# A gated cross-attention layer with a routed FFN: the end of the kernel joined into its last batch

## What is computed

```python
x = x + tanh(g_xattn) * attention(layernorm(x), ctx, ctx, mask, Wq, ..., Wo, bo)
def ffn(x):                              # x is layernorm(x) of the line above
    indices = argmax(softmax(x @ Wr + br))
    out = 0
    for i in range(8):
        xi = x * (indices == i)
        out += relu(xi @ W1[i] + b1[i]) @ W2[i] + b2[i]
    return out
x = x + tanh(g_ffn) * ffn(layernorm(x))
```

## Time and profile before

| what | value |
|---|---|
| time, three executions | 391.19, 392.97, 394.4 us (median 392.97) |
| the profiled execution: time | 391.81 us |
| its span, first to last instruction | 390.0 us |
| PE busy | 358.8 us (92% of the span) |
| DVE, ACT, POOL busy | 277.4, 247.4, 193.7 us |
| granted TensorE clock, mean over the span | 0.973 of full speed |

### The profile page before, as it was taken

One profiled execution on the slowest core, in us unless ns is written; L12 is line 12 of the kernel. 1 busy time (PEld: TensorE's weight loads), 2 busy tenths in 40 slices (PEclk: granted clock), 3 DMA queues, 4 the chain that ended last, 5 costly groups with the idle time before them and its releaser, 6 DMA issues.

```text
span 390.0 us, 11299 instructions
## 1 busy us (share of the span) xinstructions
PE 358.8 (92%) x2829; PEld 289.4 (74%) x2829; DVE 277.4 (71%) x1300; ACT 247.4 (63%) x908; POOL 193.7 (50%) x373
## 2 busy tenths in 40 slices
PE   3969998999999999999999999999999978759991
PEld 2847777677877787787778778877877757659991
DVE  3289993988598959868895989598856654645661
ACT  1767874687586758766875886677745424536670
POOL 7047363456537634673564566446643522253553
PEclk9999999999999999999999999999999975989997
DMA  7898201001100200030003002000000037333320
GB/s 211 200 366 209 87 26 60 3 2 53 61 0 0 84 27 0 0 111 0 0 2 109 0 0 90 34 0 0 0 27 3 3 114 239 115 97 90 90 60 12
DMA packets 20552, 25.21 MB, mean 65 GB/s; under 512 B 3545, under 2 KB 16677, under 8 KB 20528
## 3 DMA queue, kind: packets, MB, share of 16 engines
q1 hardware_dynamic: 18544, 19.40, 16.8%
q0 software_dynamic: 1984, 5.53, 3.9%
HBM read 18.48 MB, written 6.90 MB: 65 GB/s over the span
## 4 chain that ended last, share of the span: by engine, by line
PE 82%; DVE 4%; issue 3%; DMA 3%; ACT 3%; another core or an unknown queue 1%; DVEq 1%; SPq 1%; POOL 1%; ACTq 0%; POOLq 0%
PE ps_kv L1158 16%; PE ps_o L1158 14%; PE ps_s L1158 13%; PE ps_t L1231 12%; PE ps_w L1158 9%; PE ps_q L1158 8%; PE ps_t L1158 7%; DVE masked L752 1%; ACT prob L557 1%; DMA sorted_rows<-rows,slot_i 1%; DMA bias_rows<-in_L_ffn_b 1%; PE ps_s L1436 1%; ACT hidden L656 1%; PE ps_w L1263 1%
## 5 line engine op out<-in xcount | busy, mean ns | idle before, releaser
L422 POOL TENSOR_SCALAR prob<-prob,row_inv 128x128 f32<-128x128 f32 (+1 forms) x256 | 104.7, 428 | 138.9 <-DVE row_inv L765 138.9
L557 ACT ACTIVATE prob<-masked,neg_max 128x128 f32<-128x128 f32 (+1 forms) x256 | 113.4, 444 | 68.0 <-DVE neg_max L752 68.0
L752 DVE CUSTOM_DVE_ANT_0 masked<-ps_s,mask_now 128x128 f32<-128x128 f32 (+1 forms) x256 | 78.9, 353 | 23.8 <-PE ps_s L1158 19.7
L771 DVE COPY prob_T<-ps_t 128x384 f32<-128x384 f32 x128 | 67.4, 548 | 1.2 <-PE ps_t L1231 1.2
L1158 PE MATMUL ps_s<-k_T,q_T 64*128 64x128 f32 (+1 forms) x512 | 59.3, 350 | 1.9 <-DVE neg_max L752 1.8
L1231 PEld LDWEIGHTS ps_t<-ident,prob 128*128 128x128 f32 x384 | 41.1, 141 | 22.6 <-issue 16.8
L1231 PE MATMUL ps_t<-ident,prob 128*128 128x128 f32 x384 | 56.3, 282 | 1.5 <-DVE prob_T L771 1.3
L1158 PE MATMUL ps_o<-prob_T,v_nat 128*64 128x256 f32 (+1 forms) x512 | 55.7, 339 | 0.0
L557 ACT ACTIVATION_READ_ACCUMULATOR prob<-masked,neg_max 128x1 f32 x256 | 47.9, 187 | 0.0
L1158 PEld LDWEIGHTS ps_o<-prob_T,v_nat 128*64 128x64 f32 x512 | 31.0, 136 | 17.4 <-issue 2.1
L1158 PEld LDWEIGHTS ps_s<-k_T,q_T 64*128 64x128 f32 x512 | 33.6, 186 | 12.3 <-issue 11.1
(11 more groups left out here) (196 smaller groups left out, 574.9 us busy)
## 6 DMA issues: line engine op xcount, KB each, us to landing
ctx_buf<-in_ctx SPq DMA_DIRECT2D x8, 768.0 KB
tile_in<-sorted_rows SPq DMA_DIRECT2D x24, 128.5 KB
sorted_rows<-pad_rows POOLq DMA_DIRECT2D x6, 385.5 KB, 4.4
packs<-in_L_ffn_W SPq DMA_DIRECT2D x1, 2048.0 KB
packs<-in_L_ffn_W SPq DMA_DIRECT2D x8, 256.0 KB
ctx_nat<-in_ctx SPq DMA_DIRECT2D x8, 128.0 KB, 4.1
x_nat<-in_x SPq DMA_DIRECT2D x1, 896.0 KB, 9.1
sorted_rows<-pad_rows SPq DMA_DIRECT2D x2, 385.5 KB, 3.0
```

The lines of the kernel that those rows point to most:

```text
L422: g.tensor_scalar(prob[:, slot, lo:hi], prob[:, slot, lo:hi], row_inv[:, slot, t:t + 1], 1.0, ALU.mult, ALU.mult).then_inc(prob_ready, 1)
L557: s.activation(prob[:, slot, lo:hi], masked[:, slot % 2, lo:hi], ACT.Exp, bias=neg_max[:, slot, t:t + 1], scale=-1.0, accum_out=row_sum[:, ...
L752: v.tensor_tensor_reduce(out=masked[:, slot % 2, lo:hi], in0=ps_s[slot % 2][:, lo:hi], in1=mask_now[:, lo:hi], scale=-SCALE, scalar=FLOOR, ...
L771: v.tensor_copy(prob_T[:, slot % TSLOTS, :], ps_t[slot % 2][:, 0:W3]).then_inc(probT_kept, 1)
```

## The change

1. **Pads.** `PADS` goes from 3 to 5 tiles. `pad_at` (the places) is copied in slot 0 of the last batch, when `next_row` holds batches 0 to 5; SP sends all eight transfers. `scatter(6)` waits for them and moves on POOL from step 7 to step 5; `residual_of(7)` from step 4 to 2.
2. **Last batch, routing of batch 6.** DVE's steps are placed by tables: `second_norm` in slots 0 to 9, `choose` in 21 to 23, `place` in 27 and 28, `early_table` in 29 to 32. On PE `mean_of` moves from step 1 to 0, `mean_through_wvo` 2 to 1, `norm_transposes` 3 to 2, `router` 4 to 3, `ranks` 6 to 4, the empty products to steps 0 to 3, `REST_AT` to 4.
3. **Weights ahead.** `w1_now` and `w2_now` have 8 buffers, laid over the dead `x_nat`/`ctx_nat` and `wq_s`/`wk_s`/`wv_s`. ACT copies the first weights of tiles 0 to 4 in steps 5 and 6 of the last batch and those of 5 and 6 among the tiles; DVE copies the second weights of all seven tiles in slots 38 to 44.
4. **First tiles.** `tile_transpose(0)` comes ahead of `last_projection(7)`. SP reads the seven first rows into registers before its waits and then sends the seven loads. `LN_AT` is 3. PE finishes tile 6 before it transposes tile 7, and its loop over the 16 late tiles is written out.
5. **POOL.** Stores of tiles 0 and 1, then `scatter(7)`, then tile 2; those of tiles 3 to 6 wait also for the first products of tiles 7 to 10. The waits for the last stores move to SP.

```diff
-PADS = QT + 1
+PADS = 2 * QT + 1
...
             sp.wait_ge(pad_ready, 1)
-            for e in range(SP_PADS):
+            for e in range(E):
...
             sp.wait_ge(early_table_ready, 1)
+            early_at = [sp.value_load(tile_row[0:1, k:k + 1], min_val=0, max_val=PADROW) for k in range(EARLY)]
+            sp.wait_ge(padded, 16 * (E + 1))
+            sp.wait_ge(scattered, 16 * (NT - QT))
             for k in range(EARLY):
-                at = sp.value_load(tile_row[0:1, k:k + 1], min_val=0, max_val=PADROW)
-                if k == 0:
-                    sp.wait_ge(scattered, 16 * (NT - QT))
-                sp.dma_start(tile_in[:, k], sorted_rows[bass.ds(at, P), :]).then_inc(tile_loaded[k], 16)
+                sp.dma_start(tile_in[:, k], sorted_rows[bass.ds(early_at[k], P), :]).then_inc(tile_loaded[k], 16)
...
+            for r in range(RING):
+                sp.wait_ge(out_stored[r], 16 * (TURNS + (r < EARLY)))
...
-                    if j == 7 and not first:
+                    if j == (5 if last else 7) and not first:
+                        if last:
+                            pool.wait_ge(padded, 16 * (E + 1))
                         scatter(b - 1)
...
-            pool.wait_ge(padded, 16 * (SP_PADS + 1))
-            pool.wait_ge(pool_padded, 16 * (E - SP_PADS))
+            for tile in range(SOON):
+                store(tile, tile)
             scatter(B - 1)
-            for tile in range(EARLY):
+            store(SOON, SOON)
+            for tile in range(SOON + 1, EARLY):
+                pool.wait_ge(h_done, tile + EARLY - SOON)
                 store(tile, tile)
...
                     if last and j == REST_AT + 1:
                         keep_rest(0)
                         keep_rest(1)
+                        act.wait_ge(early_table_ready, 1)
+                        act.wait_ge(ld_ffn, 16 * (E + 2))
+                        for tile in range(2):
+                            early_w1(tile)
+                    if last and j == REST_AT + 2:
+                        for tile in range(2, 5):
+                            early_w1(tile)
...
+            def early_w2(tile):
+                if tile == 0:
+                    dve.wait_ge(early_table_ready, 1)
+                    dve.wait_ge(ld_ffn, 16 * (E + 2))
+                    dve.wait_ge(q_done, 8 * B)
+                    dve.wait_ge(kv_done, 8 * B)
+                expert = experts[tile] = expert_of(tile)
+                v.tensor_copy(w2_now[:, tile, :], packs[:, bass.ds(expert, 1), W2_AT:PACK]).then_inc(w2_ready, 1)
...
+            for tile in range(2):
+                early_rest(tile)
             for step in range(16):
                 second_norm(B - 1, step, ps_q)
...
                 if last:
+                    tile_transpose(0, 0)
                     last_projection(PAIRS - 1)
...
-EMPTY_AT = {0: (0, 1), 1: (2, 3), 2: (4,), 3: (5,), 4: (6,), 5: (7,)}
-REST_AT = 6
+EMPTY_AT = {0: (0, 1, 2), 1: (3, 4), 2: (5, 6), 3: (7,)}
+REST_AT = 4
+LAST_NORM = {0: (0,), 1: (1,), 2: (2, 3), 3: (4, 5), 4: (6, 7), 5: (8, 9), 6: (10, 11), 7: (12, 13), 8: (14,), 9: (15,)}
+LAST_CHOOSE = {21: (0, 1), 22: (2, 3), 23: (4, 5)}
+LAST_PLACE = {27: (0, 1), 28: (2, 3)}
+LAST_TABLE = {29: (0, 1), 30: (2, 3), 31: (4, 5), 32: (6, 7)}
-LN_AT = 1
+LN_AT = 3
+SOON = 2
```

More of the change, by code:

```diff
@@ L56 @@
 assert (MT - EARLY) % RING == 0 and NTILES % RING == 0
-SP_PADS = 2
 NOBODY = 1 << 20
@@ L590, in batch @@
                         context_now(b + 1)
-                    if j == 4 and not first:
+                    if j == 4 and not first and not last:
                         keep_x2T(b - 1)
@@ L1369, in batch @@
                         mean_of(b)
-                    if j == (6 if first else 2):
+                    if j == (6 if first else 1 if last else 2):
                         mean_through_wvo(b)
-                    if j == 6 and not first:
+                    if j == 6 and not first and not last:
                         ranks(b - 1)
                     if last:
+                        if j == 2:
+                            norm_transposes(b - 1, b + 1)
+                        if j == 3:
+                            router(b - 1)
+                        if j == 4:
+                            ranks(b - 1)
                         for e in EMPTY_AT.get(j, ()):
```

197 lines of the change are left out of this document (94 added, 103 removed).

## The result

The changed kernel took 390.59 us (median of 20 runs, 387.34 to 395.5) beside 393.57 us for the kernel before on the same chip (20 runs): ratio 0.9929, 95% interval 0.9908 to 0.995. That is 3.0 us gained where 7.1 were forecast, just outside the range; by the bound of 1% it is no change. The two profiled executions differ by 1.5 us (391.81 and 390.34, spans 390.0 and 388.4).

A forecast was written before the change was run, and what follows sets the result against it. PE sets the pace in the last batch and late tiles; some 15 us at most lie between. 5.8 us by tile 8 plus 1.3 at the end, 7.1, takes 392.97 to 385.9 us, likeliest 383.5 to 387.5, range 381 to 390.5.

The forecast's parts named there:

- The end: After the last store: POOL drains right behind it instead of at 386.0; 1.3 us gained if the drain keeps 3.76 us.
- The stall of `mean_of`: Step 0 of the last batch: PE waits for DVE's first layernorm step; 0.9 us, bounds 0 and 1.4.
- SP's first load: Ahead of tile 0: first load at 319.0 instead of 320.38, so tile 0 starts at 321.1, 1.4 us earlier.
- the half clock until 331: Tiles 0 to 6: PE's clock stays low until 331, so a tile takes 3.8 us there.
- Full clock: Rival, early tiles: clock doesn't fall at 317.7 or rises earlier; 12 us gained, 381 us; chance 0.12.
- my worst case: Batch 7's layernorm behind DVE's seven w2 copies: ends at 330.2 at worst, still hidden from PE.
- Tile 8 at full clock: Behind tile 7: at full clock tile 8 starts at 346.3 instead of 352.13, 5.8 us gained.
- a stop that I can't place ... I count it as gone: Ahead of tile 7's first product: ACT's unexplained 3.34 us stand vanishes, the rest of 3.9 us beyond the load's 0.3.
- the tiles keep 1.90 us: Late tiles: PE's loop written out gains nothing; tiles still follow each other every 1.90 us.
- pads late: Rival, last batch: pads land at 320.3, tile 0 starts 5 us later; 390.9 us; 0.10 with other losses.
- The stop stays: Rival, ahead of tile 8: stop from SP's first loop pass or late code remains; 4.3 us gained, 388.7; chance 0.22.
- Hidden by 0.5 us: Tiles 11 to 14: held stores' store, landing and load take 5.2 us of 5.7 available, so no wait.

The follow-up runs named there:

- b_end_on_sp: Kernel before, with SP instead of POOL waiting for the last stores; 388.4 us against 389.27, ratio 0.9968.
- the fills: Changed kernel variants with eight or sixteen unread matmuls on PE between tile 6's second product and tile 7's transpose; four runs, ratios 0.9742 to 0.9924.
- b_spaced: Kernel before, with a short POOL operation ahead of each store of tiles 0 to 6; 392.89 us against 393.47, ratio 0.9984.
- a_spaced_2: Changed kernel without the hold on stores, a short POOL operation ahead of each store of tiles 2 to 6; 386.04 us against 393.56, ratio 0.9816.
- a_again: Changed kernel untouched, measured again; 389.64 us against 393.12 for the kernel before, ratio 0.99.
- a_hold_2: Changed kernel untouched with its hold, beside variants without it; 390.36 us against 393.56 for the kernel before, ratio 0.9911.
- b_bursts: Kernel before, POOL's late loop written out, four extra indirect DMAs behind each of the stores of tiles 11 and 17; 394.97 us against 389.27, ratio 1.0127.
- a_row_late: Changed kernel without the hold, but tile 13's store held until tile 17's first product, so four stores pile up; 382.96 us against 389.85, ratio 0.9825.
- a_projection_first: Changed kernel without the hold, last piece of the output projection back ahead of tile 0's transpose; 387.83 us against 393.12, ratio 0.9872.
- the pair: Changed kernel without the hold, stores of tiles 2 to 6 unspaced and spaced, on one chip; 389.06 and 386.04 us against 393.56.

## Why the prediction was wrong

**The end: under-sized.** Forecast 1.3 us, measured in the spans 9.4 - 7.1 = 2.3 us from the last second product to the end; alone it was worth 1.2 us (b_end_on_sp). The forecast moved the drain up by 1.5 us (386.0 to 384.51) and kept its length. It began 2.4 us earlier, at 383.6, ahead of the last store's own start (383.95), and took 4.64 us instead of 3.76.

**Up to tile 7: right, in part by errors that cancel.** The stall of `mean_of` was 0.82 us (forecast 0.9). The pads were issued from 289.8 to 300.8, and each landed 4.5 us behind at the median, long before `scatter(6)`. SP's first load came at 320.02 (319.0), tile 0 at 322.21 (321.1); this last batch began 0.9 us later in the execution than the one before. A wait of 0.96 us at "rest" was not foreseen. (Two numbers of the prediction are off by a little, without weight here: by its own rows the late pads would delay tile 0 by 323.1 + 0.2 + 2.1 - 321.1 = 4.3 us and not 5, and the last step of the late table took 0.38 us before and not 0.44.) Tile 7's first product came at 344.20 (344.7). But I had kept the half clock until 331, and it was over by 319.83: tiles 0 to 6 ran at full clock. "Full clock" promised 12 us for that. About 2 us came: slots_ready at 334.5 instead of 336.8, no more, because batch 7's layernorm, behind seven copies on DVE, was done only at 329.8 (my worst case was 330.2) and PE waited 0.75 us for it. And the stop then took them back: the late table was ready at 340.5, where 341.1 was forecast.

**Tile 8 at full clock: wrong, 1.5 us.** "With it at full clock, tile 8 starts at 346.3": it did start at 346.86, but at half clock, and tile 9's transpose was 4.3 us earlier than before, not 5.8. The clock fell again behind idleness ahead of tile 7, 1.23 and 1.70 us of it, and the fills kept it up. The Trainium skill's page "TensorE: Matmul & The Clock Gate", Part 1, ties a low clock to an idle engine: here the runs agree, and the fall by 316.25 (below), with PE at work since 313.38, is one that an idle engine doesn't plainly account for.

**The step that failed: "a stop that I can't place ... I count it as gone", and with it "the tiles keep 1.90 us".** The late tiles lost 5.0 us, read from transpose to transpose against 1.90 us: 0.7 to the clock (from tile 9's to tile 10's took 2.57 us), 1.4 ahead of tile 12, whose load came late, and 2.9 around two stops (ahead of tiles 14 and 16). I had looked for what the stop waited on in the order of PE and ACT and found nothing, since it isn't there. It goes with POOL's rows of indirect DMAs, on chips that show stops at all: the spacing took it away ahead of tile 7 in b_spaced (3.45 to 0.63 us) and shortened it in a_spaced_2 (2.64 to 1.24 us). In time "pads late" (390.9) came nearest, by luck: the pads had all landed in time. Nearest in what happened was "The stop stays" (388.7), but by a wrong cause: SP's first pass or late code would have kept it ahead of tile 7, and there PE's wait shrank to 1.23 us, because the hold ends the row early. The stop itself was not gone even there: PE's signal due at 336.60 came 3.20 us late, beside PE's other work. It came back twice behind the held stores. Their price was reckoned by the buffers alone: "Hidden by 0.5 us" became a wait of 1.23 us in this profile, of 0.35 in a_again and none in a_hold_2. The term in it that was too small is the 5.2 us for store, landing and load: in this profile tile 4's store began 0.9 us behind the product that released it (349.80), landed 4.46 us later, and the load of tile 12 took 1.92 us more, 7.4 us together. That held stores pile up into rows was not priced at all.

**What isn't known.** No row was added on a chip with stops: b_bursts and a_row_late, the two runs meant for it, both fell on chips without. There the tie between row and stop rests on the runs that spaced or moved rows, with one profile of each kernel. The change with its hold was never run on a chip without stops; there the same kernel without the hold gained 6.2 and 7.7 us, on either side of the forecast's 7.1. What within the chip delays the signals, and why only on some chips, no run shows. PE's loop written out and the new order of the last batch were not tried by themselves.

## What to carry to other kernels

When a stall in the trace is released by something that the profile can't name, don't count it as gone because the order around it changes: look at what every engine, the DMA-issuing ones too, did in the 5 us ahead, and ask where that goes. A hold on stores spreads the held ones (here 1.9 to 2.6 us apart), but those that pile up behind it go out in a row, 1.29 us apart; a short operation between stores spreads them too, and it too leaves a row where POOL catches up. And compare variants side by side on one chip: 1% lay between chips here, as much as the change itself.

## What the runs showed of the hardware that I had not expected

- The kernel before ran at 389.3 and 389.9 us on two chips and at 393.1 to 393.6 on the others. Its stop and the low clock behind it cost about that difference: from tile 7's transpose to tile 9's it takes 8.16 us, and b_end_on_sp, without a stop, 3.79.
- On the chips with stops, rows of three to six of POOL's indirect DMAs, mostly 1.3 and at most 1.6 us apart, went with late signals of PE (up to 4.4 us, in a_projection_first), mostly until 1.8 to 2.8 us after the start of the last. Where they stood 1.8 us apart, the stop was shorter or absent (2.64 and 1.24 us in the pair; 3.45 and 0.63 us in the kernel before). On the chips without stops, eight in a row (a_row_late) and twenty (b_bursts) held up none of PE's work: beside a_row_late's, PE's signals came 0.01 to 0.02 us behind its products.
- PE's clock had fallen by 316.25 in a stretch in which PE was busy for 7.05 of 7.2 us, behind an idle 0.96 us and the eight-row matmuls of "rest" from 313.38, and was full again by 319.83. Before the change it had fallen by 317.98, behind the same matmuls (from 314.20) but with no idleness ahead of them and only 0.29 us just before, and was still low in the first tiles, with 3.3 idle us between the earlier trace rows.
